# Layer 1 of a four-layer graph network on one core: units of four steps with three buffers, and 28 instead of 24 of 128 tiles made by products

## The chip, the cores and the metric

The kernel runs on one core of a Trainium2 chip. The metric is the device time in microseconds; before the change it is 8717.58 us (median of three runs, 8713.29 to 8717.87).

## What is computed

Four layers over a graph with 12500 nodes of 128 features and 212500 edges, sorted by destination. Each layer gathers a row for every edge, sums the rows of each node, and ends with a residual and a layer norm. Cut to what matters here:

```
# layer 1, the one that is changed
deg = segment_sum(1, col);  dis = where(deg > 0, rsqrt(deg), 0)
agg = segment_sum(dis[row] * dis[col] * x[col], row)
x   = layernorm(x + agg + (1 + eps) * x)
# layer 0: relu(concat(x, mean of (x @ W_t)[neighbours]) @ W_u + b_u)
# layer 2: x[src] * edge_weight, summed by dst, then two dense layers
# layer 3: mish(x[src] + edge_attr @ W_e + b), summed by dst, then two dense layers
```

## The kernel before

The edges are cut into 13 supertiles (`SUP`) of 128 tiles (`T`) of 128 edges. The nodes are 98 blocks (`NB`) of 128, whose sums stand in SBUF (`acc`). Within a supertile the edges are sorted so that a walk of 225 steps, padded to 228 (`KP`), visits every pair of tile and block that can have edges in common. One step is one fp32 matmul (line 1924; the trace shows it as two instructions): the one-hot matrix `oh` of the step times the tile's 128 gathered rows, into PSUM. In layer 1 (`group_pe` with layer 1, called once for each of 19 groups of a supertile):

- A group is 12 steps (`SG`), two units of six (`US`). A unit has 768 columns in two PSUM banks; there are two such buffers. ACT fills a unit's banks with zeros (`clear_act`, line 1846), PE opens both banks with two small matmuls (lines 1771 and 1772), does six steps, and closes them with two matmuls of one column (line 1776). Then DVE adds the unit to `acc` (line 1954), where the blocks of the steps are neighbours, and makes the one-hot matrices for the unit two further on (`batch`, line 1936).
- At each group PE loads 12 registers from `tab` (`load_pe`, line 1762); they say for each step which ring slot holds the tile and which part of PSUM takes the sum.
- Of the tiles, 104 of each supertile's 128 come from DRAM by an indirect DMA on POOL (line 2014), into a ring `M1` of 55 slots (`RG`). SyncE tells PE of their arrival (`s_arr`, line 2094, counted in `arrivals_src`) and POOL of slots that are free again (`s_rel`, lines 2097 and 2100). The first supertile has all 128 gathered.
- The other 24 (`XN` = 3 of 16) are made by products. The gathered table is sorted, so a tile's rows lie in a window of 9 or 10 blocks (`WIN`, 114 in all over 12 supertiles, 9.5 on average) that ACT has loaded (`xw`). PE spreads the tile's 128 source numbers over the partitions by one matmul (`row_pe`, line 1795) into a free part of the unit's second bank, DVE compares them with the window's numbers (`row_dve`, line 1802, 1152 or 1280 columns), PE multiplies the 9 or 10 one-hot matrices with the window (line 1817), and ACT copies the sum into `M1` (line 1860). The products are called between the steps by `more`: one after each of the first five steps of an even unit and of the first two of an odd one, and all that are due at the end of the unit. A tile of products falls due every 9.5 steps.
- In unit 20 of each supertile but the last, DVE rewrites the next supertile's row of `tab` in `places` (lines 1885 to 1899), 16 instructions on one partition, since the slot of a tile depends on how many before it are products.
- From supertile 2 on, `dst_tables` makes the tables for layers 2 and 3 in pieces between the units, each on DVE (every third unit) and, one unit later, on PE (line 2173 among others).

The order on every engine is fixed by the program: a DVE unit is add, row (if one is due), batch, and then pieces or places. PE takes products of the tile x when DVE has its one-hot row (`s_ot`), and DVE writes the row for x when the products of x - 2 are done (`s_xp`). There are two `ot` buffers and two product banks (4 and 5). Bank 6 holds the numbers 0 to 127 that `batch` compares with, bank 7 serves the tables.

Of the kernel before, what the change touches and what calls it, by code (L numbers as in the profile page):

```python
# [4 lines left out]
P = 128  # L5
T = 128
# [59 lines left out]
def graph_layers(nc, x_in, src_in, dst_in, edge_in, w_in, Wt, Wu, bu, eps1, eps2, W21, b21, W22, b22,  # L66
# [22 lines left out]
    with ExitStack() as ctx:  # L89
# [38 lines left out]
        s_gx, s_ot, s_xp, s_xc, s_xw, s_map, s_clr = (sem(n) for n in ("s_gx", "s_ot", "s_xp", "s_xc", "s_xw", "s_map", "s_clr"))  # L128
# [945 lines left out]
        def fast():  # L1074
            H, US = T // 2, SG // 2
            UNITS = KP // US
            STEPS = TILES + NB - 1
# [5 lines left out]
            OH0 = [0, SUP * UNITS + 2, 2 * SUP * UNITS + 4, 2 * SUP * UNITS + 6 + 2 * KD // SG]  # L1083
            SPAN, PITCH, PACK, MARK = 8, 171, 128, 1024
            XN, XS, RG = 3, 4, 55
# [103 lines left out]
            gxf = sb("gxf", [P, 2, XT])  # L1189
            lane8, tile8 = sb("lane8", [P, 3, 8], i32), sb("tile8", [P, 3, 8], i32)  # L1190
# [49 lines left out]
            PIECES_FROM = 2  # L1240

# [513 lines left out]
            U_ALL = SUP * UNITS  # L1755
# [28 lines left out]
            PERIOD, X0 = KP / XT, KP // 2 - US * 2  # L1784
# [7 lines left out]
            def row_pe(e, x, b0):  # L1792
                s, i = x // XT + 1, x % XT
                e.wait_ge(s_gx, s)
                return e.matmul(ps[:, b0 + 1, 2 * P:3 * P], gxf[:, s % 2, i:i + 1].to_broadcast([P, P]), ident[:, :], start=False, stop=False)

            def row_dve(e, x):
                s = x // XT + 1
                b0 = 2 * ((int(due(x) // US) - 2) % 2)
                if x >= 2:  # L1800
                    e.wait_ge(s_xp, x - 1)
                e.tensor_tensor(ot[:, x % 2, 0:WIN[s], :],  # L1802
                                ps[:, b0 + 1, 2 * P:3 * P].rearrange("p (a b) -> p a b", a=1).to_broadcast([P, WIN[s], P]),
# [3 lines left out]
            def expand_pe(e):  # L1807
                for x in range(X_ALL):
                    s, i = x // XT + 1, x % XT
                    for w in range(WIN[s]):  # L1810
                        yield due(x) + (2 * PERIOD - 2 * US) * w / WIN[s]
# [25 lines left out]
            def made_in(x):  # L1837
                w = WIN[x // XT + 1]
                return -int(-(due(x) + (2 * PERIOD - 2 * US) * (w - 1) / w) // 1) // US

            def clear_act(e, u):
                h = u % 2
                e.wait_ge(s_add, ST0[1] + max(u - 1, 0) * US + 1)
                if u - 2 in ROW_UNIT:
                    e.wait_ge(s_ot, ROW_UNIT[u - 2] + 1)
                e.activation(ps_flat[:, h * 1024:h * 1024 + US * P], zwin[:, 0:1].to_broadcast([P, US * P]), ACT.Copy).then_inc(s_clr, 1)  # L1846

            def expand_act(e):
                load_window(e, 1)
                x = 0  # L1850
                for u in range(U_ALL):
                    clear_act(e, u)
                    while x < X_ALL and made_in(x) < u:
# [5 lines left out]
                        e.wait_ge(s_st, ST0[1] + (s - 1) * KP + (last // US + 1) * US)  # L1859
# [904 lines left out]
```

## Time and profile before

| | |
|---|---|
| median of three runs | 8717.58 us |
| the profiled execution | 8707.91 us, its span 8706.1 us |
| busy over the span | PE 71%, DVE 62%, ACT 43%, POOL 72% |
| mean granted TensorE clock | 0.837 |

| stage, us from the start | length | PE | DVE | ACT | POOL | clock |
|---|---|---|---|---|---|---|
| 0 to 2433: sorting, layer 0 | 2433 | 1955 | 2104 | 986 | 1717 | 0.89 |
| 2433 to 2537: end of layer 0's nodes | 104 | 63 | 89 | 84 | 61 | 0.90 |
| 2537 to 4298: layer 1, its main loop | 1761 | 1664 | 1395 | 479 | 1248 | 0.97 |
| 4298 to 4510: layer 1's nodes and the start of layer 2 | 212 | 50 | 89 | 92 | 117 | 0.56 |
| 4510 to 6460: layer 2 | 1950 | 870 | 508 | 543 | 1480 | 0.66 |
| 6460 to 8706: layer 3 | 2246 | 1599 | 1191 | 1585 | 1622 | 0.85 |

The table gives busy microseconds of each engine in each stage; stage borders are rounded. PE is TensorE's matmuls and PEld its weight loads, which overlap them; DVE is VectorE, ACT ScalarE, POOL GpSimd, SP SyncE, and a q behind an engine's name its sequencer. The ends of matmuls are modelled, so PE counts as busy in short gaps as well; the starts of weight loads tell more.

### The profile page before, as it was taken

How to read it: one execution, taken by the hardware profiler on the slowest of the kernel's cores; microseconds unless marked ns; L12 is line 12 of the kernel's file. 1: busy time of each engine (PE TensorE's matmuls, PEld its weight loads, DVE VectorE, ACT ScalarE, POOL GpSimd, SP SyncE). 2: the span in 40 equal slices, each digit the busy share in tenths (PEclk: the TensorE clock that was granted, in tenths of full speed). 3: DMA queues.
4: the chain of work that ended last, by engine and by line, in shares of the span. 5: the costliest groups of instructions: out<-in, count | busy, mean ns of one | idle time of the engine just before them, and what ended most of it. 6: DMA issues, size and time to landing. Idle time of an engine off the chain costs nothing. (4 is left out here: it accounts for less than half of the span.)

```text
span 8706.1 us, 153774 instructions
## 1 busy us (share of the span) xinstructions
PE 6202.1 (71%) x41943; PEld 5309.4 (61%) x41944; DVE 5376.6 (62%) x10966; ACT 3768.3 (43%) x8055; POOL 6245.2 (72%) x6523
## 2 busy tenths in 40 slices
PE   5788888888869999999634444444446777777776
PEld 2566666657769898999633333333336666666665
DVE  8898898888877888877722222222225555555554
ACT  5445355342052222222422222222236777777775
POOL 3677777777757766777477777777767777777774
PEclk7899999998789999999866666666668888888887
DMA  1122122121142222222222222222223443334432
GB/s 35 43 52 52 51 52 52 51 52 49 44 130 63 57 52 54 54 56 55 77 64 64 60 64 60 64 64 60 64 64 105 110 110 110 108 110 109 111 108 71
DMA packets 575365, 611.58 MB, mean 70 GB/s; under 512 B 114414, under 2 KB 472474, under 8 KB 574618
## 3 DMA queue, kind: packets, MB, share of 16 engines
q0 software_dynamic: 203776, 417.74, 18.9%
q1 hardware_dynamic: 294120, 145.77, 5.8%
q10 hardware_dynamic: 76722, 38.13, 1.5%
q8 instruction: 466, 7.63, 0.4%
q14 instruction: 281, 2.30, 0.1%
HBM read 562.68 MB, written 38.51 MB: 69 GB/s over the span
## 5 line engine op out<-in xcount | busy, mean ns | idle before, releaser
L2014 POOL DMA_INDIRECT M<-in_x,ixb x1664 | 1696.3, 1019 | 538.5 <-issue 530.0
L2195 PE MATMUL ps<-M,oh 128*128 x7056 | 1285.8, 349 | 1064.5 <-ACT M L2550 1034.1
L2061 POOL DMA_INDIRECT M<-t,ixb x1664 | 1615.7, 971 | 503.9 <-issue 498.1
L2195 PEld LDWEIGHTS ps<-M,oh 128*128 128x128 f32 x7056 | 1194.0, 253 | 1240.1 <-issue 1176.3
L2061 POOL DMA_INDIRECT M<-x,ixb x1664 | 1577.5, 948 | 503.9 <-issue 503.1
L2014 POOL DMA_INDIRECT M_any<-t,ixb x1376 | 1302.3, 946 | 501.1 <-issue 445.4
L1435 ACT ACTIVATE oht<-oneh,ot 128x128 f16<-128x128 f16 x3264 | 965.3, 387 | 979.6 <-DVE oneh L1411 979.6
L2213 DVE TENSOR_TENSOR acc<-acc,ps 128x1024 f32 x294 | 357.9, 1217 | 1587.5 <-PE ps L1776 1587.5
L1954 DVE TENSOR_TENSOR acc<-acc,ps 128x774 f32 (+1 forms) x988 | 942.7, 954 | 570.7 <-PE ps L1776 542.5
L2550 ACT ACTIVATE M<-M,wD 128x128 f32<-128x128 f32 x1664 | 517.1, 388 | 1488.2 <-DMA M<-x,ixb 1473.2
L1924 PEld LDWEIGHTS ps<-M,oh 128*128 128x128 f32 x5928 | 894.5, 209 | 266.0 <-issue 160.3
L1924 PE MATMUL ps<-M,oh 128*128 x5928 | 999.8, 311 | 66.8 <-DVE oh L1936 29.3
L1924 PE MATMUL ps<-M_any,oh 128*128 x5928 | 1024.4, 293 | 29.1 <-issue 22.4
L1936 DVE TENSOR_TENSOR oh<-ps,relS 128x768 f32<-128x768 f32 x992 | 941.0, 949 | 1.9 <-DVEq L1482 0.2
L2252 PE MATMUL ps<-we_sb,et 128*128 128x128 f32 x3328 | 558.8, 337 | 491.4 <-DVE M L2296 464.6
L1924 PEld LDWEIGHTS ps<-M_any,oh 128*128 128x128 f32 x5928 | 841.0, 197 | 90.6 <-issue 56.6
L1817 PE MATMUL ps<-xw,ot 128*128 128x128 f32 x5472 | 882.0, 283 | 0.0
L2296 DVE TENSOR_TENSOR M<-M,ps 128x512 f32<-128x512 f32 x416 | 267.4, 684 | 960.5 <-DMA M<-t,ixb 960.3
L2252 PEld LDWEIGHTS ps<-we_sb,et 128*128 128x128 f32 x3328 | 518.1, 245 | 515.2 <-issue 356.1
L1846 ACT ACTIVATE ps<-zwin 128x768 f32<-128x768 bf16 x494 | 401.6, 813 | 990.6 <-DVE ot L1802 658.3
L1817 PEld LDWEIGHTS ps<-xw,ot 128*128 128x128 f32 x5472 | 728.0, 193 | 0.0
L1771 PE MATMUL ps<-ones_b,zwin 128*128 128x471 bf16 (+2 forms) x1282 | 427.9, 334 | 225.1 <-DVE acc L2213 128.2
(306 smaller groups left out, 9256.1 us busy)
## 6 DMA issues: line engine op xcount, KB each, us to landing
er<-in_edge_attr SPq DMA_DIRECT2D x414, 256.0 KB
M<-in_x,ixb POOLq DMA_INDIRECT x1664
M<-x,ixb POOLq DMA_INDIRECT x1664
M<-t,ixb POOLq DMA_INDIRECT x1664
M_any<-t,ixb POOLq DMA_INDIRECT x1376
x<-lay SPq DMA_DIRECT2D x48, 256.0 KB, 2.4
part<-x ACTq DMA_DIRECT2D x48, 256.0 KB, 4.6
lay<-in_x SPq DMA_DIRECT2D x24, 256.0 KB, 3.9
```

What stands on the lines that cost most here:

```text
L1435: ins = e.activation(oht[:, r, k, w * P:(w + 1) * P], oneh[:, r, k, :], ACT.Copy, scale=pf[:, 8 * c + k:8 * c + k + 1])
L1771: e.matmul(ps[:, b0, 0:n0], zwin[:, 0:1].to_broadcast([P, P]), ones_b[:, 0:1].to_broadcast([P, n0]), start=True, stop=False)
L1817: ins = e.matmul(ps[:, 4 + x % 2, 0:P], ot[:, x % 2, w, :], xw[:, (FIRST[s] + w) % XR, :], start=w == 0, stop=w == WIN[s] - 1)
L1846: e.activation(ps_flat[:, h * 1024:h * 1024 + US * P], zwin[:, 0:1].to_broadcast([P, US * P]), ACT.Copy).then_inc(s_clr, 1)
L1924: ins = e.matmul(ps_flat[:, bass.ds(slot * pitch + b0 * 512, width)], oh[:, j, :], tile_at(ring, tile, width), start=False, stop=False)
L1936: e.tensor_tensor(oh[:, u * US:u * US + US, :], ps[:, bank, 0:P].rearrange("p (a b) -> p a b", a=1).to_broadcast([P, US, P]), rel[:, k:k + ...
L1954: e.tensor_tensor(to, to, ps_flat[:, h * 1024:h * 1024 + US * pitch].rearrange("p (a b) -> p a b", b=pitch)[:, :, 0:width], ALU.add).then_ ...
L2014: e.indirect_dma_start(M1[:, m1_slot(s, t), :] if layer else M[:, t % RING, 0:P], None, table[0:rows, :], bass.IndirectOffsetOnAxis(ap=ixb ...
L2061: e.indirect_dma_start(M2[:, t % RING, :], None, table[:, :], bass.IndirectOffsetOnAxis(ap=ixb[:, t:t + 1], axis=0)).then_inc(s_g[n % 16], 16)
L2195: ins = e.matmul(ps_flat[:, bass.ds(slot * P, P)], oh[:, j, :], tile_at(M2, tile, P), start=False, stop=False)
L2252: ins = e.matmul(ps[:, 5 + h, j * P:(j + 1) * P], et[:, h, j * P:(j + 1) * P], we_sb[:, :], start=True, stop=True)
L2550: ins = e.activation(M2[:, t % RING, :], M2[:, t % RING, :], ACT.Copy, scale=wD[:, t:t + 1])
```

## The change

In layer 1 a unit has four steps (`U4`) in one bank, and there are three buffers (`B4`), in banks 0 to 2; a group is three units. A unit is opened by one matmul, and its last step closes it. The row of a product's numbers has bank 3 for itself, with semaphores of its own (`s_row`, and PE waits for `s_ot` of the row before). ACT's clearing no longer waits for the row's reader. 28 of the 128 tiles (7 of 32) are made by products, in supertiles 1 to 12, and 100 gathered; the ring has 51 slots, which with the 28 places for products are the same 79 slots. A tile of products falls due every 8.14 steps, its products are spread over 4.3 steps instead of 7, and its row is asked for three units of four steps ahead instead of two of six. `places` computes the blocks of the units anew, since four steps start at other blocks than six: 21 instructions instead of 16, in unit 30 of 57; DVE reads a unit's first block from `first4`. `window_rows` takes 7 small instructions instead of 3. A piece of the tables is due every fourth unit (`piece_due`), for PE one unit later as before. Layer 0 keeps its code, taken out of the shared function.

```
-            XN, XS, RG = 3, 4, 55
+            XN, XS, RG = 7, 5, 51
+            U4, B4 = 4, 3
+            def piece_due(s, u):
+                return s >= PIECES_FROM and 0 <= u < UNITS4 - 1 and u % 4 == 0
...
-            ROW_UNIT = {int(due(x) // US) - 2: x for x in range(X_ALL)}
+            ROW_UNIT = {int(due(x) // U4) - B4: x for x in range(X_ALL)}
...
+            def row_pe(e, x):
                 s, i = x // XT + 1, x % XT
                 e.wait_ge(s_gx, s)
+                if x:
+                    e.wait_ge(s_ot, x)
+                e.matmul(ps[:, 3, 0:P], gxf[:, s % 2, i:i + 1].to_broadcast([P, P]), ident[:, :], start=True, stop=True).then_inc(s_row, 1)
...
+            def clear_act(e, u):
+                e.wait_ge(s_add, ST0[1] + max(u - B4 + 1, 0) * U4 + 1)
+                e.activation(ps[:, u % B4, :], zwin[:, 0:1].to_broadcast([P, U4 * P]), ACT.Copy).then_inc(s_clr, 1)
...
-            PLACES = 12 + 2 * ((GT + RG - 2) // RG)
+            PLACES = 17 + 2 * ((GT + RG - 2) // RG)
...
+            def group4_pe(e, regs, s, m, more):
...
+                for h in range(B4):
+                    u, k = s * UNITS4 + B4 * m + h, s * KP + m * SG + h * U4
+                    if u in ROW_UNIT:
+                        row_pe(e, ROW_UNIT[u])
+                    e.wait_ge(s_clr, u + 1)
+                    e.matmul(ps[:, h, 0:P], zwin[:, 0:1].to_broadcast([P, P]), ones_b[:, :], start=True, stop=False)
+                    if h == 0:
+                        e.wait_ge(s_arr, ready + (s * T + ARR0 + TILES))
+                    e.wait_ge(s_oh, OH0[1] + u + 1)
+                    for j in range(U4):
+                        tile, slot = at[h * U4 + j]
+                        ins = e.matmul(ps_flat[:, bass.ds(slot * P + h * 512, P)], oh[:, h * U4 + j, :], tile_at(M1_any, tile, P),
+                                       start=False, stop=j == U4 - 1)
+                        if j < U4 - 1:
+                            more(k + j, 1)
+                    ins.then_inc(s_st, U4)
+                    more(k + U4 - 1, KP)
...
+            def unit4_dve(e, regs, left, s, u):
...
+                e.wait_ge(s_st, ST0[1] + k0 + U4)
+                e.wait_ge(s_add, ST0[1] + k0 + 1)
+                e.tensor_tensor(to, to, ps[:, h, :].rearrange("p (a b) -> p a b", b=P), ALU.add).then_inc(s_add, U4)
+                if s * UNITS4 + u in ROW_UNIT:
+                    row_dve(e, ROW_UNIT[s * UNITS4 + u])
+                batch(e, h, relS, k0 + SG, 6, U4)
...
-                        if s + 1 < SUP and u == 20:
+                        if s + 1 < SUP and u == 30:
                             places(e, tm, s + 1)
```

## Rows read from the trace of the kernel before

**Rows 1.** Busy time by stage: stretch, length, busy us (instructions) per engine, clock, DMA.

```profile
3716.00:4116.00 400.00, 384.15 (x3314) 367.89 (x3314) 316.32 (x358) 112.19 (x187) 293.68 (x316) 0.98 0.21 55
```

**Rows 2.** Waits, 2537 to 4298: who waited for whom, us in total, times, longest.

```profile
DVE acc L1954 <- PE ps L1776: 338.7, 295, 7.4
...
PEld ps L1771 <- ACT ps L1846: 51.4, 29, 11.7
...
POOL M_any L2014 <- SPq L2100: 28.3, 28, 4.7
POOL M_any L2014 <- SPq L2097: 25.5, 29, 6.5
...
PEld ps L2173 <- DVE seld L2172: 18.1, 13, 4.2
```

**Rows 3.** Groups by line, 2537 to 4298: count | busy, mean ns | idle before, releaser.

```profile
L2014 POOL DMA_INDIRECT M_any<-t,ixb x1312 | 1241.5, 946 | 481.3 <-issue 426.3 <-SPq L2100 28.3 <-SPq L2097 25.5
L1924 PE MATMUL ps<-M_any,oh 128*128 x5928 | 1024.4, 293 | 29.1 <-issue 22.4 <-SPq L2094 0.7
...
L1954 DVE TENSOR_TENSOR acc<-acc,ps 128x768 f32 x494 | 470.1, 952 | 351.3 <-PE ps L1776 338.7 <-issue 11.8
...
L1802 DVE TENSOR_TENSOR ot<-ps,iota_ps 128x1280 f32<-128x1280 f32 x144 | 213.7, 1484 | 3.0 <-PE ps L1817 2.7
```

**Rows 4.** Timeline of DVE, the first instruction of places(): start, length, engine and line.

```profile
2877.59 0.26 DVE L1885 TENSOR_SCALAR tmr<-tab 1x228 int32<-1x228 int32 x1
...
3716.16 0.43 DVE L1885 TENSOR_SCALAR tmr<-tab 1x228 int32<-1x228 int32 x1
...
4116.10 0.26 DVE L1885 TENSOR_SCALAR tmr<-tab 1x228 int32<-1x228 int32 x1
```

**Rows 5.** Timeline, 3901 to 3906: an odd unit, its products, the next group's start.

```profile
3901.39 0.10 PEld L1771 LDWEIGHTS ps<-ones_b,zwin 128*128 128x128 bf16 x1
3901.51 0.10 PEld L1772 LDWEIGHTS ps<-ones_b,zwin 128*128 128x128 bf16 x1
3901.56 0.30 PEld L1795 LDWEIGHTS ps<-ident,gxf 128*128 128x128 f32 x2
3901.79 1.42 PEld L1924 LDWEIGHTS ps<-M_any,oh 128*128 128x128 f32 x12
3903.13 0.21 PEld L1776 LDWEIGHTS ps<-ones_b,zwin 128*128 128x128 bf16 x2
3903.27 1.42 PEld L1817 LDWEIGHTS ps<-xw,ot 128*128 128x128 f32 x12
...
3903.53 0.95 DVE L1936 TENSOR_TENSOR oh<-ps,relS 128x768 f32<-128x768 f32 x1
3904.40 0.94 DVE L1954 TENSOR_TENSOR acc<-acc,ps 128x768 f32 x1
...
3904.60 0.10 PEld L1771 LDWEIGHTS ps<-ones_b,zwin 128*128 128x128 bf16 x1
...
3905.30 0.30 PEld L1924 LDWEIGHTS ps<-M_any,oh 128*128 128x128 f32 x2 [0.48 <-issue]
```

**Rows 6.** Timeline, 3849 to 3864: places() on DVE and PE behind it.

```profile
3849.34 0.26 DVE L1885 TENSOR_SCALAR tmr<-tab 1x228 int32<-1x228 int32 x1
...
3855.13 0.94 DVE L1954 TENSOR_TENSOR acc<-acc,ps 128x768 f32 x1
...
3858.43 0.10 PEld L1771 LDWEIGHTS ps<-ones_b,zwin 128*128 128x128 bf16 x1 [3.71 <-ACT ps L1846]
...
3858.77 2.63 PEld L1924 LDWEIGHTS ps<-M_any,oh 128*128 128x128 f32 x12 [0.21 <-issue]
...
3861.57 2.21 PEld L1817 LDWEIGHTS ps<-xw,ot 128*128 128x128 f32 x10
```

**Rows 7.** Line 1762, 2537 to 4298: count, ns min/median/max, first and last start.

```profile
L1762 PEldq TENSOR_LOAD <-tab x247: 843/848/1026, 2542.2 to 4296.1; - x124
```

**Rows 8.** The page's costliest groups: additions of 1024 and of 512 columns on DVE.

```profile
L2213 DVE TENSOR_TENSOR acc<-acc,ps 128x1024 f32 x294 | 357.9, 1217 | 1587.5 <-PE ps L1776 1587.5
...
L2296 DVE TENSOR_TENSOR M<-M,ps 128x512 f32<-128x512 f32 x416 | 267.4, 684 | 960.5 <-DMA M<-t,ixb 960.3
```

**Rows 9.** Timeline near the loop's end, where no products are made: starts of two even units.

```profile
4272.79 0.10 PEld L1771 LDWEIGHTS ps<-ones_b,zwin 128*128 128x128 bf16 x1 [0.93 <-issue]
...
4278.83 0.10 PEld L1771 LDWEIGHTS ps<-ones_b,zwin 128*128 128x128 bf16 x1 [0.50 <-ACT ps L1846]
```

More of the change, by code:

```diff
@@ L1076, in fast @@
             UNITS = KP // US
+            U4, B4 = 4, 3
+            UNITS4 = KP // U4
+            assert SG == U4 * B4 and UNITS4 * U4 == KP
             STEPS = TILES + NB - 1
@@ L1850, in expand_act @@
                 x = 0
-                for u in range(U_ALL):
+                for u in range(U_ALL4):
                     clear_act(e, u)
@@ L1896, in places, with group_pe @@
                 op(lambda: e.scalar_tensor_tensor(c0, c0, float(RG), one, ALU.add, ALU.mult))
-                op(lambda: e.tensor_tensor(at, at, t, ALU.subtract))
                 op(lambda: e.tensor_tensor(at, at, c0, ALU.add))
+                op(lambda: e.tensor_tensor(blocks, iotaK[0:1, 0:KP], t, ALU.subtract))
+                op(lambda: e.tensor_scalar(blocks, blocks, float(NB - 1), None, ALU.min))
+                op(lambda: e.tensor_scalar(starts, every(blocks, U4), float(NB - U4), None, ALU.min))
+                op(lambda: e.tensor_tensor(blocks.rearrange("p (m w) -> p m w", w=U4), blocks.rearrange("p (m w) -> p m w", w=U4),
+                                           starts.rearrange("p (m w) -> p m w", w=1).to_broadcast([1, UNITS4, U4]), ALU.subtract))
+                op(lambda: e.scalar_tensor_tensor(at, blocks, float(PACK), at, ALU.mult, ALU.add))
+                op(lambda: e.tensor_scalar(row, row, 10, 10, ALU.logical_shift_right, ALU.logical_shift_left))
                 op(lambda: e.tensor_tensor(row, row, at, ALU.add))
-            def group_pe(e, layer, regs, s, m, more=None):
-                ring, width, pitch = (M, W1C, PITCH) if layer == 0 else (M1_any, P, P)
+                assert tm.n == PLACES * (s + 1)
+            def group_pe(e, regs, s, m):
                 if m == 0:
-                    if layer:
-                        e.wait_ge(s_map, PLACES * (s + 1))
                     load_pe(e, regs, 0, s * KP)
-                at, ready = steps_pe(e, regs, T - 1 if layer else RING - 1)
+                at, ready = steps_pe(e, regs)
                 u0 = s * UNITS + 2 * m
@@ L2431, in run_vector @@
                 e.wait_ge(s_v, tv.n)
-                for u in range(2):
-                    batch(e, u, relS, u * US, 6)
+                for u in range(B4):
+                    batch(e, u, relS, u * U4, 6, U4)
                 pieces = dst_tables(e, "v", tv, tp, ta)
                 for s in range(SUP):
-                    for u in range(UNITS):
-                        drain(unit_dve(e, 1, regs, left, s, u))
+                    for u in range(UNITS4):
+                        unit4_dve(e, regs, left, s, u)
                         if (s, u) == (0, 0):
@@ L2480, in period @@
                     for m in range(KI):
-                        for u, _ in enumerate(group_pe(e, 0, regs, s, m)):
+                        for u, _ in enumerate(group_pe(e, regs, s, m)):
                             if 2 * m + u:
@@ L2509, in run_tensor @@
                     for m in range(KI):
-                        for h, _ in enumerate(group_pe(e, 1, regs, s, m, more)):
+                        for h, _ in enumerate(group4_pe(e, regs, s, m, more)):
                             if (s, m, h) == (PIECES_FROM, 0, 0):
                                 e.wait_ge(s_ld, NLATE)
-                            if s >= PIECES_FROM and (2 * m + h) % 3 == 1:
+                            if piece_due(s, B4 * m + h - 1):
                                 next(pieces, None)
```

93 lines of the change are left out of this document (46 added, 47 removed).

## The prediction

> **What bounds the kernel now.** I first cut the span into stages and looked for the one that the edit touches: layer 1's main loop, from 2537 to 4298 us. In its steady part PE shows busy for 384 of 400 us at nearly full clock, DVE for 316, POOL for 294 [rows 1]. Two engines look full, so busy shares don't decide. The waits of the loop do [rows 2]. POOL waits for the ring's releases (SyncE lines 2097 and 2100) for 28.3 + 25.5 us: its ring of rows is full again and again, and the consumer is late. The opposite wait, PE's first step waiting for SyncE's arrival count (line 2094), is 0.7 us in 1761 [rows 3]. So the gathers, though 104 of them at 946 ns and 0.30 us of issue make 130 us of every supertile [rows 3], don't set the end; the PE side does.
>
> The marks at which DVE writes a supertile's tables of places (unit 20 of each supertile) give the period: (4116.10 - 3716.16) / 3 = 133.3 us, and (3716.16 - 2877.59) / 6 = 139.8 us while the tables for the destination layers are also made [rows 4].
>
> What fills 133.3 us on PE I price from starts of weight loads, which stand back to back [rows 5]. Six steps take 3901.79 to 3903.13, 0.223 each. Six products take 3903.27 to 3904.60, 0.222 each. The two closing matmuls of a unit take 3903.13 to 3903.27, 0.14. The two clears take 3901.39 to 3901.56, 0.17; a row takes 3901.56 to 3901.79, 0.23. A supertile has 228 steps (50.9), 24 x 9.5 = 228 products (50.6), 24 rows (5.5), 38 closes (5.3) and 38 pairs of clears (6.5): 118.8 us. Once in a supertile PE stands still for 3.71 us, because DVE spends 3849.34 to 3855.13 on the 16 small instructions of places(); after it the next 12 step loads take 2.63 us instead of 1.42 and the next 10 product loads 2.21 instead of some 1.2, the half clock, so 2.2 us more [rows 6]. That leaves 133.3 - 118.8 - 3.7 - 2.2 = 8.6 us a supertile, 0.45 us for each of the 19 groups of 12 steps. Two things are in it. The registers are loaded by an instruction that holds PE's sequencer for 848 ns a group [rows 7]. And the sequencer waits for the one-hot tiles: DVE's batch ends at 3904.48 (3903.53 + 0.95), and the first step's load starts at 3905.30 behind a gap of 0.48 [rows 5].
>
> **The change, part by part, per supertile.**
> (a) 28 instead of 24 tiles by products: 4 x 9.5 = 38 more products x 0.222 = +8.4, 4 rows x 0.23 = +0.9 on PE. POOL issues 4 gathers less, 4 x 1.25 = 5 us, 60 us in all; as POOL isn't what ends last, this is worth nothing.
> (b) Units of four steps in one bank: the closes go, 38 x 0.14 = -5.3. Clears: 57 single ones instead of 38 pairs. The first of a pair holds 0.12 (3901.39 to 3901.51 is its load; 0.17 holds both) so 57 x 0.11 = 6.3 for 6.5: -0.2. Sum of (a) and (b): +3.8.
> (c) DVE: 57 adds and 57 batches of 512 elements for 38 of 768. The row for 512 is 684 ns and that for 1024 is 1217 [rows 8], so 267 ns are for each 256 elements and some 150 are fixed; 951 for 768 fits [rows 3]. Successive operations overlap by 0.08 (3903.53 to 3904.40 for 0.95 us), so 0.07 of the fixed part is paid: 38 x 0.07 = 2.7 us. Four more one-hot rows at 1.40 are 5.6. DVE goes from 105 us to about 114 of a period over 130: not the bound by itself. Nine more loads of DVE's registers for the units hide behind a running batch; uncovered they would be below 0.85 us each [rows 7].
> The Trainium skill, VectorE: DVE Perf Modes, section "The TRN2 errata", speaks against smaller tiles: a fixed latency is exposed between instructions, and many small tiles pay it each time. By it the whole 150 ns would count, 5.7 us instead of 2.7; the trace's overlap says less, and neither is on PE's path.
> (d) Three buffers instead of two. The batch for a unit is made three units ahead (12 steps as before, but after a short unit), and the clear no longer waits for the row's reader. This can give back of the 8.6 us what is waiting for DVE, not what is register loading, of which there are still 19. The bounds are 0 and 8.6; a load of 0.85 with 0.18 to 0.3 behind it exceeds what a flush of products covers by 0.2 to 0.3, so about 5 us stays anyhow. I take 2.8.
> (e) places(): one instruction less and six more, 21 instead of 16. At 5.79 / 16 = 0.36 each that is 1.8, DVE away for 7.6 us. Cover: before, PE has two units of 3.45 us; now three of 2.3, but a row's matmul waits (new) for the one-hot row two units back, and behind it on PE's queue stand the clear and the steps of its unit, on which DVE's next add waits. With rows in units 31 and 33 PE does two units (4.7 us) and stands until 1.5 (add, batch) + 7.6 + 0.6 (add) + 1.4 (one-hot row) = 11.1 + 0.1: 6.5 us. With rows in 30, 32, 34 it is three units (7.0) against 13.7: 6.7. So 6.6 for 3.7: +2.9. Bounds: 0 (if only the clear counted, the third unit covers the added 1.8) and +4.
> (f) The making of the destination tables meets PE and DVE one unit apart; waits for them at line 2173 alone are 18.1 us [rows 2]. The unit in between is 2.3 instead of 3.45 us, DVE's part before it shrinks by 2 x 0.27 = 0.54: 0.6 us less cover in some 49 meetings, about half of them with a one-hot row in the way. Bounds 0 and 29; I take +8 in all.
> (g) The first 102 and last 126 steps have no products. There two units take 4272.79 to 4278.83, 6.04 us, of which 12 steps are only 2.7 on the array: PE's sequencer sets the pace, clears wait 0.5 us at most, and DVE isn't what is late [rows 9]. Registers per step and loads per group stay, so 0; bounds -10 and +5. Ring 51 instead of 55 loses 4 rows of 946-ns gathers of depth, on an engine that has 5 us more room: 0. ACT clears 512 columns 57 times instead of 768 38 times; it is idle for more than half: 0.
> Layer 0 and layers 2 and 3 keep their instructions, so the loop's difference is the kernel's.
>
> **Sum.** 3.8 - 2.8 + 2.9 = +3.9 a supertile, times 12 supertiles with products = +47, and +8: +55 us. The profiled execution took 8707.9, its span 8706.1, which would be 8761; the median of the runs is 8717.6, 0.11% above it, so **8773 us**.
>
> **The rivals.** About 0.2%, 17 us, is what a measurement of this kernel tells from no change.
> 1. The third buffer takes all 8.6 (faster). For it: the sequencer stands at batches, and DVE's chain of add 0.87, row 1.40, batch 0.95, then 0.8 to the first step, then a unit, is nearly as long as two units. Against it: the 848-ns load is in there too. From a return of 5.9 a supertile the other side begins: 3.8 - 8.6 + 2.9 = -1.9, times 12 = -23, 8695; if the pause stays at 3.7 as well, -4.8 x 12 = -58, 8660. Chance 0.22.
> 2. POOL is the bound after all (faster): 48 x 1.25 = 60 off, 8658. Against it stands the 0.7 us of waiting for arrivals. 0.03.
> 3. The one bank for rows becomes the loop (slower). From a row's matmul: 0.33 with the clear, four steps and up to three products between them 1.45, 0.3 to DVE, add 0.6, one-hot row 1.4, 0.2 back: 4.3 us for two units, and 5.0 where a group's register load falls in. PE's own work is 122.6 / 57 x 2 = 4.3. Two chains of one length hinder each other; 0.35 more a group gives 6.7 more a supertile, +80 on the forecast: 8853. 0.20.
> 4. No difference: the third buffer returns 6.5, which pays for all but 0.2 of the rest: 8720. 0.13.
> 5. The forecast, 8745 to 8810: 0.42.
>
> The range must reach into 1 and into 3: 8685 to 8853 leaves out about half of the first two rivals and the upper part of the third, some 0.2. Faster 0.25, same 0.13, slower 0.62.
>
> **What would show it.** The period between the marks of places(): 137 us (forecast), 131 or less (rival 1), 143 (rival 3). The pause of PE behind places(): 6 to 7 us, now ended by the one-hot row. POOL's waits for releases larger than 54 us, as its work shrinks; if they vanish, rival 2. In the last 60 us no change. Wrong would be the forecast if PE's gaps at the start of groups go, or if the half clock appears at more places than one a supertile. On that clock, the rows show the half level after a pause of 3.71 us. The Trainium skill, TensorE: Matmul & The Clock Gate, section "What's actually happening", says that the default is the slow clock and that activity releases it; here the trace agrees with 2.63 us for 1.42.

## The result, and the profile after

The changed kernel takes 9029.6 us (median; 9021.8 to 9032.2) where the kernel before takes 8717.7: a ratio of 1.0357, 95% interval 1.0339 to 1.0375. That is 312 us more, and outside the range forecast. The profiled execution has a span of 9025.6 us against 8706.1, 319.5 us more, both at a granted clock of 0.837.

Where the time went is plain from the first and last row matmul (row_pe), which stand in every supertile that has products. Below is the view of that line in the profile before, then after (count, ns min/median/max, first and last start).

```profile
L1795 PEld LDWEIGHTS ps<-ident,gxf x576: 192/192/337, 2583.7 to 4220.5; 128*128 128x128 f32 x192
```
```profile
L1805 PEld LDWEIGHTS ps<-ident,gxf x672: 185/188/338, 2583.0 to 4525.9; 128*128 128x128 f32 x168
```

Layer 1's loop starts at the same time and is 1942.9 us long between the two rows instead of 1636.8: 306 of the 319.5 us between the two profiles lie there; the rest comes behind the loop, in layers 2 and 3, whose instructions the change leaves alone. There are 336 rows now, so one every 5.80 us.

The stretch that [rows 1] showed before, in the profile after (stretch, length, busy us of PE, PE weight loads, DVE, ACT and POOL, then clock, DMA share, GB/s):

```profile
3716.00:4116.00 400.00, 352.87 (x2811) 328.99 (x2810) 302.36 (x448) 96.04 (x218) 243.56 (x262) 0.97 0.18 47
```

Every engine is less busy than before: PE 353 of 400 us for 384, POOL 244 for 294, DVE 302 for 316. No engine became the bound by its work, so the time is in waits. The waits of the loop, 2537 to 4614 us, after (who waited for whom, us in total, times, longest), which answer [rows 2]:

```profile
DVE acc L2000 <- PE ps L1953: 432.1, 411, 6.2
...
POOL M_any L2056 <- SPq L2139: 231.3, 73, 11.2
POOL M_any L2056 <- SPq L2142: 131.9, 44, 8.5
PEld ps L1805 <- issue: 127.1, 141, 6.2
...
PE ps L1805 <- DVE ot L1812: 101.0, 95, 6.0
DVE ot L1812 <- PE ps L1827: 89.3, 132, 1.8
...
PEld ps L2215 <- DVE seld L2214: 53.0, 24, 7.0
```

POOL waits for the ring 363 us instead of 54, so the gathers are further from the bound than before. PE stands before the row matmul (line 1805) until DVE has written the one-hot row of the tile before it, which didn't occur before. DVE in its turn stands before a one-hot row (line 1812) until the products of two tiles earlier have read that buffer: 132 times and 89.3 us, where before it was 22 times and 5.0 us in all (2.7 of them in [rows 3]). PE's wait for the destination tables, 18.1 us before [rows 2], is 53.0.

**The budget of PE.** The next three fences show where the time of PE's weight loads went in the part of the loop with products, by line: count, busy us and mean ns, then idle time just before them; the last line of each is the whole stretch. First the kernel before, 2604 to 4250 us:

```profile
L1924 PEld LDWEIGHTS ps<-M_any,oh 128*128 128x128 f32 x5491 | 769.4, 194 | 72.8 <-issue 46.1
...
L1771 PEld LDWEIGHTS ps<-ones_b,zwin 128*128 128x128 bf16 x457 | 45.6, 100 | 43.5 <-ACT ps L1846 38.4 <-issue 2.6
...
L2173 PEld LDWEIGHTS ps<-seld,rowf 128*128 128x128 f32 x54 | 8.5, 199 | 18.1 <-DVE seld L2172 18.1
...
2604.00:4250.00 1646.00, 1564.49 (x13396) 1489.91 (x13394) 1323.81 (x1645) 449.61 (x744) 1198.72 (x1286) 0.98 0.22 56
```

Then the changed kernel, 2608 to 4560 us:

```profile
L1953 PEld LDWEIGHTS ps<-M_any,oh 128*128 128x128 f32 x5504 | 816.7, 196 | 133.0 <-issue 104.2
L1805 PEld LDWEIGHTS ps<-ident,gxf 128*128 128x128 f32 x662 | 102.9, 194 | 129.0 <-issue 125.6
L1947 PEld LDWEIGHTS ps<-ones_b,zwin 128*128 128x128 bf16 x688 | 69.7, 101 | 31.9 <-issue 19.5 <-ACT ps L1853 11.0
L2215 PEld LDWEIGHTS ps<-seld,rowf 128*128 128x128 f32 x54 | 8.6, 201 | 53.0 <-DVE seld L2214 53.0
...
L2181 PEld LDWEIGHTS ps<-ident,gff 128*128 128x128 f32 x13 | 1.9, 147 | 23.1 <-DVE gff L2180 23.0
...
2608.00:4560.00 1952.00, 1683.80 (x13263) 1568.50 (x13263) 1456.82 (x2257) 453.33 (x1021) 1154.10 (x1237) 0.96 0.17 45
```

And the experiment e17 (below), which has the change's units, tiles and buffers but not its waits, 2608 to 4226 us:

```profile
L1972 PEld LDWEIGHTS ps<-M_any,oh 128*128 128x128 f32 x5507 | 794.7, 192 | 88.9 <-issue 62.5
L1805 PEld LDWEIGHTS ps<-ident,gxf 128*128 128x128 f32 x662 | 100.3, 192 | 4.3 <-issue 3.7
...
L2234 PEld LDWEIGHTS ps<-seld,rowf 128*128 128x128 f32 x54 | 8.1, 189 | 12.9 <-DVE seld L2233 12.7
...
2608.00:4226.00 1618.00, 1566.38 (x13258) 1501.52 (x13257) 1423.84 (x2251) 453.94 (x1022) 1226.41 (x1241) 1.00 0.21 55
```

With the smaller groups of the same views the sums close:

| PE's weight loads, us | before | after | e17 |
|---|---|---|---|
| busy | 1489.9 | 1568.5 | 1501.5 |
| idle before steps | 72.8 | 133.0 | 88.9 |
| idle before row matmuls | 0 | 129.0 | 4.3 |
| idle before clears and closes | 55.4 | 31.9 | 5.3 |
| idle before the tables' matmuls | 27.8 | 90.0 | 18.0 |
| sum | 1645.9 | 1952.4 | 1618.0 |

Of 306 us, 228 are waiting and 79 are busy time. Of the busy time 67 us are not work either: e17 issues the same PE instructions in 67 us less, at a granted clock of 1.00 instead of 0.96. The clock's own records of these stretches have 150 us at the lower of the two levels (1.2 instead of 2.4 GHz), in 26 pieces, against 65 us in 13 pieces before and 7 us in e17. In 150 us PE does half of what it could, so 75 us at most are lost by it. Thirteen of the 26 pieces, 106 us together, lie at the 13 pauses of PE of more than 3 us.

**One turn of the new chain**, a timeline of the changed kernel (start, length, engine, line, and the wait before it):

```profile
3100.32 0.30 PEld L1805 LDWEIGHTS ps<-ident,gxf 128*128 128x128 f32 x2
...
3101.10 0.30 PEld L1953 LDWEIGHTS ps<-M_any,oh 128*128 128x128 f32 x2 [0.46 <-issue]
...
3102.66 1.20 PEld L1827 LDWEIGHTS ps<-xw,ot 128*128 128x128 f32 x10
...
3103.08 0.69 DVE L2000 TENSOR_TENSOR acc<-acc,ps 128x512 f32 x1 [2.02 <-PE ps L1953]
...
3103.77 0.10 PEld L1947 LDWEIGHTS ps<-ones_b,zwin 128*128 128x128 bf16 x1
...
3104.15 1.49 DVE L1812 TENSOR_TENSOR ot<-ps,iota_ps 128x1280 f32<-128x1280 f32 x1 [0.39 <-PE ps L1827]
...
3105.56 0.68 DVE L1964 TENSOR_TENSOR oh<-ps,relS 128x512 f32<-128x512 f32 x1
3105.76 0.30 PEld L1805 LDWEIGHTS ps<-ident,gxf 128*128 128x128 f32 x2 [0.46 <-issue]
```

PE makes a row at 3100.32, runs its unit and the five products behind it (ten weight loads, two for each) until 3103.77. DVE adds the unit from 3103.08 on, 2.76 us after the row, and is free for the one-hot row 0.39 us before it starts, but its buffer is still read by those products. It starts at 3104.15 and takes 1.49, and 0.12 later, at 3105.76, comes the next row matmul, which stood 0.46 us. One turn is 5.44 us; on average it is 5.80, and in e17 the rows stand (4191.9 - 2585.0) / 335 = 4.80 apart.

**The block of places()**, same kernel:

```profile
4096.25 0.26 DVE L1893 TENSOR_SCALAR tmr<-tab 1x228 int32<-1x228 int32 x1
...
4103.68 0.67 DVE L2000 TENSOR_TENSOR acc<-acc,ps 128x512 f32 x1
...
4107.15 0.50 PEld L1805 LDWEIGHTS ps<-ident,gxf 128*128 128x128 f32 x2 [5.78 <-issue]
...
4108.17 0.55 PEld L1827 LDWEIGHTS ps<-xw,ot 128*128 128x128 f32 x2
```

DVE is away for 7.43 us, PE stands 5.78 until a one-hot row, and then a pair of loads takes 0.55 instead of 0.30.

### The profile page after: what moved, and what is told of

Read it like the earlier page. It is cut to its first block and busy times, and to the rows that moved or that the text cites. A ratio compares the mean times of both kernels' runs of the same rounds, so it can differ in the third digit from the quotient of the medians.

```text
span 9025.6 us, 155105 instructions
## 1 busy us (share of the span) xinstructions
PE 6300.6 (70%) x41497; PEld 5389.5 (60%) x41717; DVE 5510.8 (61%) x11622; ACT 3775.0 (42%) x8350; POOL 6213.6 (69%) x6475
## 5 line engine op out<-in xcount | busy, mean ns | idle before, releaser
L2056 POOL DMA_INDIRECT M_any<-t,ixb x1328 | 1258.0, 947 | 816.4 <-issue 452.2
L1953 PE MATMUL ps<-M_any,oh 128*128 x5928 | 1138.2, 297 | 71.2 <-issue 62.9
L1827 PE MATMUL ps<-xw,ot 128*128 128x128 f32 x6384 | 1051.1, 280 | 0.0
L1953 PEld LDWEIGHTS ps<-M_any,oh 128*128 128x128 f32 x5928 | 885.6, 198 | 153.3 <-issue 115.3
L1964 DVE TENSOR_TENSOR oh<-ps,relS 128x512 f32<-128x512 f32 (+1 forms) x1240 | 975.9, 787 | 1.9 <-DVEq L1490 0.2
L1827 PEld LDWEIGHTS ps<-xw,ot 128*128 128x128 f32 x6384 | 893.6, 197 | 0.0
L2000 DVE TENSOR_TENSOR acc<-acc,ps 128x512 f32 x741 | 506.7, 684 | 433.4 <-PE ps L1953 432.1
L1867 ACT ACTIVATE M_any<-ps 128x128 f32<-128x128 f32 x336 | 93.3, 278 | 1295.9 <-PE ps L1827 1285.6
L1981 DVE TENSOR_TENSOR acc<-acc,ps 128x774 f32 x494 | 471.9, 955 | 223.6 <-PE ps L1784 209.6
```

The lines of the kernel that those rows point to most:

```text
L1827: ins = e.matmul(ps[:, 4 + x % 2, 0:P], ot[:, x % 2, w, :], xw[:, (FIRST[s] + w) % XR, :], start=w == 0, stop=w == WIN[s] - 1)
L1953: ins = e.matmul(ps_flat[:, bass.ds(slot * P + h * 512, P)], oh[:, h * U4 + j, :], tile_at(M1_any, tile, P), start=False, stop=j == U4 - 1)
L1964: e.tensor_tensor(oh[:, u * n:u * n + n, :], ps[:, bank, 0:P].rearrange("p (a b) -> p a b", a=1).to_broadcast([P, n, P]), rel[:, k:k + n]. ...
L1981: e.tensor_tensor(to, to, ps_flat[:, h * 1024:h * 1024 + US * PITCH].rearrange("p (a b) -> p a b", b=PITCH)[:, :, 0:W1C], ALU.add).then_in ...
L2000: e.tensor_tensor(to, to, ps[:, h, :].rearrange("p (a b) -> p a b", b=P), ALU.add).then_inc(s_add, U4)
L2056: e.indirect_dma_start(M1[:, m1_slot(s, t), :] if layer else M[:, t % RING, 0:P], None, table[0:rows, :], bass.IndirectOffsetOnAxis(ap=ixb ...
```

## The experiments

Two kinds of chips came up, and no number below can be read without it. On the one (e14 to e17) the kernel before takes 8714 us, as in the result above; call it **A**. On five others (e1 to e13 and e18) it takes 11153 to 11254 us; call it **B**. DVE's operations take the same time on both (a one-hot row 1487 ns, an addition 684). On B the work of PE is signalled late again and again. In the loop of e6 the signals of 265 of 682 units come more than 1.5 us after the recorded end of the unit's last matmul (an end that is modelled), 9.2 us at most; in the changed kernel's trace on A none of 682 does. PE's weight loads have 129 gaps over 1.5 us in the loop of e6, 500 us together, against 35 gaps and 124 us on A. The engines behind PE show waits that the trace can't assign ("remote"), as this one of e6; in the profiles on A no row of the loop has "remote". What delays the signals stays open.

```profile
DVE acc L2000 <- remote: 383.2, 108, 13.6
```

Each run is compared with runs of the kernel before on the same chip. "Loop" is the time from the first to the last row matmul in its profile; on A it is 1637 for the kernel before and 1943 after.

| run | kernel | chip | ratio (95%) | loop, us | PE idle at rows, us |
|---|---|---|---|---|---|
| e6 | changed | B | 1.0207 (1.0174-1.0240) | 2516 | 432.5 |
| e14 | changed | A | 1.0353 (1.0336-1.0371) | 1941 | 127.9 |
| e11, e15 | batches read SBUF | B, A | 1.0072 (1.0044-1.0101), 1.0346 (1.0329-1.0364) | 2328, 1942 | 330.2, 128.1 |
| e1, e8 | changed, 24 tiles | B | 1.0076 (1.0046-1.0105), 1.0084 (1.0055-1.0112) | 2337, 2364 | 279.8, 256.2 |
| e3 | rows later | B | 1.0150 (1.0116-1.0183) | 2384 | 348.5 |
| e12 | batch first | B | 1.0194 (1.0172-1.0216) | 2443 | 431.7 |
| e4, e7, e18 | two row banks | B | 0.9950 (0.993-0.997), 0.9950 (0.9931-0.997), 0.9938 (0.9915-0.9962) | 2202, 2238, 2186 | 27.4, 27.0, 25.4 |
| e10 | two banks, rows later | B | 0.9937 (0.9913-0.9960) | 2182 | 23.4 |
| e13 | two banks, places spread | B | 0.9941 (0.9917-0.9964) | 2168 | 28.8 |
| e17 | all three | A | 0.9966 (0.9953-0.9978) | 1607 | 3.7 |
| e2, e9 | before, 28 tiles | B | 1.0061 (1.0037-1.0084), 1.0046 (1.0028-1.0064) | 2287, 2339 | 13.5, 13.4 |
| e5 | before, places spread | B | 0.9998 (0.9984-1.0011) | 2225 | 1.7 |
| e16 | before, batches read SBUF | A | 1.0085 (1.0068-1.0102) | 1650 | 0 |

**The control**, the changed kernel unedited.

> The changed kernel itself, as the control for what runs beside it. Measured so far: 9029.6 us, ratio 1.036 to the kernel before on a chip on which the latter takes 8718 us. The five kernels run so far beside a kernel before that takes 11167 us all stayed within 1.5% of it, with PE standing 4 to 5 us at a time, without a wait, far more often than in the profiles of before and after. Theory P (the cost of the change is waits between PE and DVE, and stalls of PE alone hide them): where before takes about 8720 this gives 1.034 to 1.038; where it takes about 11170 it gives under 1.02. Rival (the cost is work, which stalls don't hide): +312 us on either, which is 1.028 of 11170.

> The changed kernel again, as the control for the batches' source. It had ratio 1.0207 (1.0174 to 1.0240), and the loop from the first to the last row matmul took 2516 us in its profile. Theory C (the gap of 150 us between it and the kernel that only reads the batches' constant row from SBUF is a chance of one call, since PE's stalls without a wait fall differently in each program and call): ratio 1.010 to 1.016 here. Theory S (the source itself): 1.018 to 1.023 again.

On A the result comes back to 0.04% (e14's own expectation was written for B). On B the ratio is 1.0207, just above what was expected, and +257 us instead of 305: PE's late signals there cover only a small part of the cost. At line 1805 PE even stands longer than on A, 432.5 us for 127.9.

**The parts one by one.** Only the ring and the tiles:

```diff
-            XN, XS, RG = 7, 5, 51
+            XN, XS, RG = 3, 4, 55
```

> The changed kernel (units of four, three buffers, own bank for rows) with 24 product tiles and a ring of 55 as before. Chain theory (the changed kernel's loss is the chain one-hot row of tile x <- products of tile x-2, which are flushed at the end of the row's own unit <- row matmul <- one-hot row of x-1): a tile falls due every 9.5 instead of 8.1 steps, so the chain has 2.4 units and not 2.0 for each turn; most of the 312 us go, 8760 to 8830. Array theory (the 456 additional products are what costs): the same or less, 8720 to 8760. Short-unit theory (every unit of four pays fixed waits whatever the tiles are): the loss stays, 8950 or more.

> The changed kernel with 24 tiles by products instead of 28 (ring 55): units of four, three buffers and the row bank alone. Theory P (rows follow each other every 2.4 units instead of 2.0, so the row bank seldom makes PE wait): on a chip where before takes about 8720, ratio 1.005 to 1.018. Rival (the cost lies in the units of four: 19 clears of tables and 57 adds and batches for 38): ratio above 1.025.

and, in the kernel before, the same line the other way.

> The kernel before with 28 product tiles and a ring of 51, units of six and two buffers kept. Array theory: most of the 312 us appear here, 8950 or more. Chain theory: 38 more products a supertile at 0.22 us and four more one-hot rows; in units of six the row is made when the products of two tiles before are long done, so 8720 + 12 x (4 to 9) = 8770 to 8830. Short-unit theory: near 8770 too.

> The kernel before with 28 tiles by products (ring 51) and nothing else of the change. 4 rows and 38 products more a supertile on PE are 8.4 + 0.9 us by 12, +112 us, if PE bounds all of the loop, and less as far as they fit into its gaps of 8.6 us a supertile: on a chip where before takes about 8720, ratio 1.006 to 1.016. Rival (the products cost what they take and the rows' one-hots push DVE past PE as well): 1.02 and more.

e6, e8 and e9 ran on one chip. The 28 tiles alone cost 0.46% there, the units of four with the third buffer and the row bank alone 0.84%, both together 2.07%. So the two halves of the change don't add up: 0.8% come on top. With 24 tiles a row comes every 57 / 24 = 2.4 units instead of 2.0, and the idle time before rows falls from 432 to 256 us; in the kernel before, with 28 tiles, it is 13. So four additional tiles cost little in the kernel before, with units of six and a row's place in each unit's bank (0.46%), and more in the changed kernel, with one bank for all rows (1.0207 for 1.0084).

**A second row bank**, with the batches' constant row moved to SBUF, since that frees bank 6:

```diff
-                if x:
-                    e.wait_ge(s_ot, x)
-                e.matmul(ps[:, 3, 0:P], gxf[:, s % 2, i:i + 1].to_broadcast([P, P]), ident[:, :], start=True, stop=True).then_inc(s_row, 1)
+                if x >= 2:
+                    e.wait_ge(s_ot, x - 1)
+                e.matmul(ps[:, 3 + 3 * (x % 2), 0:P], gxf[:, s % 2, i:i + 1].to_broadcast([P, P]), ident[:, :], start=True, stop=True).then_inc(s_row, 1)
...
-                batch(e, h, relS, k0 + SG, 6, U4)
+                batch(e, h, relS, k0 + SG, None, U4)
```

> The changed kernel with two PSUM banks for rows in turn (3 and 6; VectorE reads the numbers 0 to 127 from SBUF instead of bank 6), so that a row matmul waits for the one-hot row of x-2 and not of x-1. VectorE's wait for the products stays. Chain theory: the 127 us at the row matmul vanish, but the next link takes over part of it: 8920 to 8980. If the single bank alone were the cause: under 8880. Array theory: no change.

> The changed kernel with two banks for rows, 3 and 6 in turn (the batches read their constant row from SBUF), so that a row's matmul waits for the one-hot before last. Theory P, that the single row bank sets the pace (PE stands before row matmuls for 129 of the 316 us by which the loop grew, at line 1805): on a chip where before takes about 8720, 130 to 220 us come back, 8810 to 8900, ratio 1.011 to 1.021. Rival F (DVE is late because it waits for the products of the flush, and PE would wait for the batch behind it in the same place): under 60 us come back, above 8970. Where before takes about 11170 nothing above 1% is expected to be told apart.

> The changed kernel with two row banks alone, once more. Measured beside a kernel before of 8714 us: the changed kernel 1.0353, all three edits together (two banks, rows later, places spread) 0.9966, a gap of 336 us. Theory P (the single bank is nearly all of the 336): where before takes about 8720, ratio 0.999 to 1.006, the other two edits being worth 20 to 80 us together. Rival (the products that hold the one-hot's buffer, or the block of places(), carry a third or more): 1.010 or above. Where before takes about 11200: 0.995 as twice before.

The wait table of e6 and of e7, both on one chip:

```profile
PEld ps L1805 <- issue: 432.5, 218, 7.2
```
```profile
PEld ps L1947 <- ACT ps L1853: 157.0, 66, 11.5
...
PEld ps L1805 <- issue: 27.0, 43, 2.3
```

One edit takes 405 of 432 us of standing away, and the loop falls by 278 us. The other 127 us come back in another place: PE's wait for the clear (line 1947) is 157.0 us, and was 30.2 in e6. On three chips the kernel is then faster than the kernel before instead of slower. The expectation of e7, that on B nothing above 1% could be told apart, missed. On B every kernel with two banks lies between 0.9937 and 0.9950, and every changed kernel with one bank between 1.0072 and 1.0207.

**Or is it the batches' source?** Half of that edit alone:

```diff
-                batch(e, h, relS, k0 + SG, 6, U4)
+                batch(e, h, relS, k0 + SG, None, U4)
```

> The changed kernel with its one row bank, and only the other half of the edit of the two banks: the batches read their constant row from SBUF. It tells whether the gain of the two banks came from the second bank or from the batches' source. Theory P (the bank): ratio 1.018 to 1.023, as the changed kernel. Rival (reading bank 6 of PSUM from DVE while PE writes others cost the time): under 1.005.

> The changed kernel with its one row bank and only the batches' constant row read from SBUF, again (it had ratio 1.0072, 1.0044 to 1.0101, and a loop of 2328 us between the first and last row matmul). Theory S: 1.005 to 1.010 again, and at least 1% below the changed kernel beside it. Theory C: 1.010 to 1.018, within 0.5% of the changed kernel beside it.

> The kernel before with the batches of layer 1 made from the constant row in SBUF instead of bank 6, and nothing else. Theory S (reading that bank costs something of its own): ratio 0.988 to 0.995. Theory C or P (it costs nothing; a batch took 681 ns from PSUM and 684 from SBUF): 0.998 to 1.002.

e11 missed the expectation for the bank: 1.0072 looked as if half the gain came from the source. On A, beside the changed kernel, it is 1.0346 for 1.0353, and the loops are 1942 and 1941 us: the source gives nothing. The gap on B lies between two different chips and is therefore the measure of how far a size on B can be trusted, about 1.3%. On B the bank can be told from the source on one chip: e10 and e13 read SBUF as e11 does, have the second bank and one small edit each, and stand at 0.9937 and 0.9941 beside e11's 1.0072, with PE idle before rows for 23.4 and 28.8 us instead of 330.2. In the kernel before, the source even costs 0.85%, outside both expectations of e16, but mostly not where it was edited: the loop is 13 us longer, while its first row comes at 2642 us instead of 2584, after a stage that has no edited instruction. In the other five profiles on A it comes between 2573 and 2585 us. No run here explains those 59 us.

Two rows in halves of one bank, which would have left bank 6 alone, were not tried.

**Which wait is it, and in which order?** Rows made two units ahead instead of three, so that the products have left the buffer when DVE comes:

```diff
-            ROW_UNIT = {int(due(x) // U4) - B4: x for x in range(X_ALL)}
+            ROW_UNIT = {int(due(x) // U4) - 2: x for x in range(X_ALL)}
```

> The changed kernel with one number changed: the row of a product tile is made two units of four ahead of its due step and not three. The products of tile x-2 are then done when VectorE comes to the row of x. Chain theory: VectorE's 89 us of waiting for products at the one-hot row fall under 15, TensorE's 127 us of waiting at the row matmul fall by more than half, and the time to 8850 to 8900. Array theory and short-unit theory: no change, within 20 us of 9030.

> The changed kernel with two row banks, and each row made two units ahead of its products instead of three. Beside a kernel before of 11254 us the changed kernel had ratio 1.0207, two banks alone 0.995, rows later alone 1.015. Theory P: two separate waits, PE's for the row bank and DVE's for the products that still read the one-hot's buffer (124 us of DVE waits are left with two banks, most of them behind PE's own stalls): both edits together give 0.990 to 0.995, no worse than two banks alone. Rival (with the row later, its one-hot becomes late for its products, and PE waits there): above 0.998.

In e3 DVE's wait for the products is gone (its trace has no wait at line 1812), and PE still stands 348.5 us before rows: the wait for the buffer may lengthen the chain but doesn't make it. With two banks the edit is worth nothing that can be told from e4, e7 and e18.

The batch ahead of the one-hot row on DVE:

```diff
-                if s * UNITS4 + u in ROW_UNIT:
-                    row_dve(e, ROW_UNIT[s * UNITS4 + u])
                 batch(e, h, relS, k0 + SG, 6, U4)
+                if s * UNITS4 + u in ROW_UNIT:
+                    row_dve(e, ROW_UNIT[s * UNITS4 + u])
```

> The changed kernel with one row bank, where DVE makes the batch of one-hots for the unit three ahead before it makes a row's one-hot, not behind it. Theory P (PE stands for the row bank): the row's one-hot comes 0.68 us later, the 28 row matmuls of a supertile wait as much or more: ratio 1.018 to 1.030. Rival F (PE stands because batches are queued behind a one-hot that waits for products): ratio under 1.012.

1.0194, as the theory of the bank has it, and PE stands before rows for 431.7 us. Had it stood for batches queued behind a one-hot row, this edit would have helped; it didn't, so PE stands for the one-hot row itself. Whether making that row later costs anything isn't shown: e11 on the same chip has 1.0072 and 330.2 us but differs in the batches' source too, and the unedited changed kernel, on another chip, has 1.0207 and 432.5 us.

**The block of places().** Its operations one to a unit (in the kernel before from unit 16 on, in the changed one from unit 24):

```diff
-                        if s + 1 < SUP and u == 30:
-                            places(e, tm, s + 1)
+                        if s + 1 < SUP and u == 24:
+                            placing = places(e, tm, s + 1)
+                        if s + 1 < SUP and 24 <= u:
+                            for _ in range(1):
+                                next(placing, None)
```

> The kernel before with the 16 instructions of places() spread over units 16 to 31, one behind each unit, instead of all behind unit 20. If TensorE's pause of 3.7 us and the half clock behind it (2.2 us) are the price of places() in one piece, and nothing else is late in its place: 12 x 3 to 5.9 us less, 8650 to 8682 against 8718. If the time only moves to the group starts (VectorE is then a little late 16 times): 8700 to 8720.

> The changed kernel with two row banks, and the 21 operations of places() spread one to a unit from unit 24 on, instead of one block of 7.5 us on DVE in unit 30. In the changed kernel's trace that block is followed by one wait of PE of 6 to 7 us a supertile at a table's matmul. Theory: 3 to 6 us a supertile, 35 to 70 us of 11200 come back: ratio 0.988 to 0.993. Rival (the block is paid by DVE's slack as in the kernel before, where spreading it gave 0.9998): 0.994 to 0.997.

On B neither moved the time: e5 0.9998, and e13 0.9941 beside 0.9938 to 0.9950 for two banks alone, which is the rival's figure.

**All three edits**, on A:

> The changed kernel with two row banks, rows made two units ahead and places() spread one operation to a unit. Two banks alone had 0.995, with rows later 0.9937, with places spread 0.9941. Theory (the waits are separate): 0.989 to 0.993. Rival (what is left in the loop is PE's own work, so that a third wait removed gives nothing): 0.9935 to 0.995.

8682.3 us against 8713.6, ratio 0.9966. This is faster than both kernels, though less so than either expectation, both drawn from B. Its loop is 1607 us, 30 shorter than before and 334 shorter than e14's. In its steady part PE is busy for 393 of 400 us at a clock of 1.00, and in all of the loop's part with products no pause over 3 us is left. The stretch of [rows 1] in e17:

```profile
3716.00:4116.00 400.00, 392.75 (x3360) 378.91 (x3360) 350.99 (x527) 115.68 (x263) 308.07 (x312) 1.00 0.21 54
```

The 8.6 us a supertile on which the forecast's third term rested are not all gone: PE still idles 88.9 us before steps, 72.8 before the change. What the bank alone would give on A no run shows, since e18, meant for it, fell on a chip of kind B; the same holds for rows later and places() spread, each alone.

## Why the prediction was wrong, by its own steps

The direction was right, and so was the place: the loop of layer 1, with POOL further off the bound. The size was off by 257 us. The step that failed is the price of the one row bank: in the sum the wait before row matmuls stood at 0, and only rival 3 had it, at 80 us. It measured 75 us at the rows alone, and with it the gain of 34 us that (d) took from the third buffer came out as 61 us of loss. The terms over 12 supertiles, and what they measured:

| term | forecast | measured | from |
|---|---|---|---|
| (a) + (b) work | +46 | about +38 | e17's busy 1501.5 less before's 1489.9 without its half clock of 12 x 2.2 |
| (d) third buffer | -34 | steps +60, clears about +1.5 | idle columns; clears without pauses over 3 us |
| (e) places(), the pauses | +35 | +40 | 13 pauses over 3 us, 77.9 us, for 10 with 37.6 |
| half clock | 0 | about +41 | 67 (after less e17) less 26 |
| (f) tables | +8 | +51 | without pauses over 3 us: 65.8 for 15.1 |
| row matmuls | 0 | +75 | 129.0 less the 9 pauses over 3 us in it, 53.7 |
| sum | +55 | +306 | |

(The pauses are counted in the records behind the idle columns.)

**(a), (b), (e) and (g) held.** The new work is 38 us for 46. The steps behind the last row of the loop, for which (g) had 0, take 76.0 us for 75.6. The pause behind places() was forecast as 6.5 to 6.7 us, ended by a one-hot row; the twelve of them are 6.2 us on average, 5.78 in the timeline above, and nine end with a one-hot row, the other three, up to 7.1 us, with a table's matmul. What (e) left out is that a pause has a tail, though [rows 6] had shown it. The slower loads behind it were priced once for before and not again for the longer pauses. The forecast had named the half clock at more places than one a supertile as a sign of being wrong, and it came: 26 pieces in twelve supertiles.

**(d) failed, and with it the choice of the likeliest case.** Step (d) took from the 8.6 us a supertile of idle time a gain of 2.8, as if DVE's lead over PE grew with the number of buffers. The lead counts only if nothing else orders the two. The single row bank does so every second unit: PE may not make a row before DVE has written the one-hot row before it. Idle time before steps, from which (d) expected its gain, rose from 72.8 to 133.0 us. In e17, with the bank doubled, rows later and the block spread, idle time before steps, clears and closes is 94.2 us instead of 128.2. That looks like the -34 of (d), but 24.9 of the 128.2 us are seven pauses over 3 us behind places(), which (e) counts. Without them it is 103.3, so that -9 is left, and before steps alone e17 idles 16 us more than the kernel before. So (d) was put too high even where the one bank isn't in the way; with the bank it became a loss.

**Rival 3 was the right mechanism, with a link missing and a stretch priced too low.** It priced the row chain as 0.33 + 1.45 + 0.3 + 0.6 + 1.4 + 0.2 = 4.3 us for two units, the same as PE's own work, and from it drew 8853 with a chance of 0.20. The chain as measured turns in 5.44 us above, and a row comes every 5.80 us on average. In the 142 turns of the changed kernel's trace in which PE stands 0.1 to 3 us before the next row, the parts are on average 2.73 us from a row's matmul to the addition (forecast 0.33 + 1.45 + 0.3 = 2.08), 0.69 for the addition (0.6), 0.45 of waiting for products (0), 1.43 for the one-hot row (1.4) and 0.31 back (0.2). So two parts were wrong. The larger one is the stretch in which PE runs its unit, 0.65 us longer than priced; in the turn above 0.46 us of it is a stand before the steps. The other is the wait that stands in row_dve itself and that the chain left out: the one-hot row of x can't be written until the products of x - 2 have read the buffer, and the last of these are in the flush behind the same unit, five products in 1.20 us. In the kernel before, a row's place lies in its unit's bank and two units of six steps lie between; the wait was 5.0 us in all, and I took it to stay there. How much of the loss this link carries stays open: without it e3 has 1.0150, with it the one-bank kernels on B have 1.0072 to 1.0207, and the chips differ by about 1.3%. That the single bank closes the loop is shown on B (e6 and e7, one chip, 432.5 and 27.0 us). On A, where the forecast was measured, only the three edits together show it, 128 us to 4, and how the 306 us divide among them there is not shown.

**(f) was the same fault in small.** The forecast had two engines that meet at tables with 0.6 us less cover. Where DVE already runs late because of rows, each meeting adds its lateness: 53.0 for 18.1 us at one line (35.9 for 9.9 without the pauses over 3 us), and back to 12.9 in e17, with the same tables and units as short.

**The range.** The waits were each priced alone, with the others at rest. They share the two engines: a late one-hot row makes its batch late, the batch the steps, the steps the next addition, and that the clear. +75 at rows come with +60 at steps, +51 at tables and +41 of clock. Rival 3's end of 8853 was the price of one of these waits; the range should have reached to the sum of all that hang on the same loop. A smaller slip: the times of rivals 1 and 4 (8695 and 8720) leave out the +8 of (f).

Of the forecast's signs, the period between the marks of places() was to tell the cases apart: 137 for the forecast, 143 for rival 3. The marks after (timeline of DVE) answer [rows 4]:

```profile
3784.93 0.26 DVE L1893 TENSOR_SCALAR tmr<-tab 1x228 int32<-1x228 int32 x1
...
4404.51 0.26 DVE L1893 TENSOR_SCALAR tmr<-tab 1x228 int32<-1x228 int32 x1
```

(4404.51 - 3784.93) / 4 = 154.9 us. Rivals 1, 2 and 4 are refuted by it, and so is rival 3's size.

## What to carry to other kernels

When a private place for a hand-over (a region in each unit's bank) is made into one shared place, write out the closed loop it makes between the two engines, with every wait on the way, also those that are worth nothing today; if its time is about that of the engine's own work, it decides, and a deeper buffer elsewhere, as the third one here, may then bring nothing. Two places instead of one turned +3.5% into -0.3% here together with two small edits. And price a wait with the others moved: where two in-order engines wait for each other at several places in turn, one loop that is too long shows up as idle time at all of them.

## What the runs showed of the hardware

Chips differ in a way that no duration of DVE's operations shows. On five the same program took 28% longer (11167 for 8718 us), with DVE's operations as long as ever (684 ns for an addition in e6 and in the changed kernel's profile on A); in the loop of e6 the signals of PE's units come late, 265 of 682 by more than 1.5 us, and the cause is open. Experiments there kept the sign of the bank's effect on three chips but not sizes: the two kernels that are 0.07% apart on one chip of kind A were 1.3% apart on two of kind B. So compare only kernels that ran beside each other.

Short pauses cost more than their idle time. The changed kernel's 13 pauses over 3 us are 78 us of idle time, and at them lie 106 us at the lower clock; another 31 us at the lower clock lie at shorter pauses of 1.5 to 3 us. In all the same PE instructions take 67 us longer than in e17, where no pause over 3 us is left and the granted clock is 1.00.

An edit that touches only layer 1's instructions (e16) came with a first row matmul at 2642 us instead of 2584. It is one profile, and unexplained.
